# Cross attention: exponentials head by head from the score banks, with the maximum as bias and the sums as a by-product

## The reference

```
def _L1_xattn_ref(query, key, value, Wq, bq, Wk, bk, Wv, bv, Wo, bo, ln_gamma, ln_beta):
    N_HEAD, MODEL_DIM, KEY_DIM, VALUE_DIM = (16, 256, 64, 64)
...
    residual = query
    q = (query @ Wq + bq).reshape(b, sq, N_HEAD, KEY_DIM)
    k = (key @ Wk + bk).reshape(b, key.shape[1], N_HEAD, KEY_DIM)
    v = (value @ Wv + bv).reshape(b, value.shape[1], N_HEAD, VALUE_DIM)
    scores = jnp.einsum('bqhd,bkhd->bhqk', q, k) / TEMP
    attn = jax.nn.softmax(scores, axis=-1)
    out = jnp.einsum('bhqk,bkhd->bqhd', attn, v).reshape(b, sq, N_HEAD * VALUE_DIM)
    out = out @ Wo + bo + residual
    mu = jnp.mean(out, axis=-1, keepdims=True)
    var = jnp.var(out, axis=-1, keepdims=True)
    return (out - mu) * jax.lax.rsqrt(var + EPS) * ln_gamma + ln_beta
```

## Time and profile before

| | |
|---|---|
| median of three runs | 976.95 us (976.56 to 977.26) |
| profiled execution, its time | 975.6 us |
| its span | 973.8 us |
| TensorE busy in the span | 839.3 us, 86% |
| weight loads | 698.3 us, 72% |
| VectorE | 603.9 us, 62% |
| ScalarE | 398.8 us, 41% |
| GpSimd | 223.8 us, 23% |
| mean granted TensorE clock | 0.944 of 2.4 GHz |

### The profile page before, as it was taken

How to read it: one execution, slowest core, us unless ns; L and a number is a source line. 1 busy time by engine, 2 the same in 40 slices (tenths; PEclk the granted TensorE clock), 3 DMA queues, 4 the chain that set the end, 5 groups by cost and what they waited for, 6 DMA issues and landing times.

```text
span 973.8 us, 14784 instructions
## 1 busy us (share of the span) xinstructions
PE 839.3 (86%) x4805; PEld 698.3 (72%) x4806; DVE 603.9 (62%) x1275; ACT 398.8 (41%) x815; POOL 223.8 (23%) x324
## 2 busy tenths in 40 slices
PE   4777999988689999967899979999997059999996
PEld 3456888755578886644788858888886059999996
DVE  4565888747468887573677668899984403333332
ACT  1555667636456765234455523333331002222321
POOL 3771000035300000200001113555453521111111
PEclk9997999999779999989899989999999579999999
DMA  9100000000000000611000073000000264554540
GB/s 290 38 1 0 1 2 1 1 1 1 1 1 1 1 1 1 224 42 52 18 0 0 1 243 103 1 0 1 1 1 1 93 234 144 174 195 166 181 141 8
DMA packets 31624, 57.54 MB, mean 59 GB/s; under 512 B 3285, under 2 KB 22517, under 8 KB 31445
## 3 DMA queue, kind: packets, MB, share of 16 engines
q1 hardware_dynamic: 28339, 49.41, 15.6%
q0 software_dynamic: 2640, 7.30, 2.1%
q10 hardware_dynamic: 594, 0.19, 0.1%
HBM read 47.06 MB, written 8.21 MB: 57 GB/s over the span
## 4 chain that ended last, share of the span: by engine, by line
PE 63%; DVE 17%; issue 6%; ACT 5%; POOL 5%; DMA 2%; SPq 1%; DVEq 0%; ACTq 0%; POOLq 0%
PE PS L1867 9%; PE PS L700 8%; PE PS L1878 8%; PE PS L744 6%; PE PS L1152 4%; PE PS L1286 4%; PE PS L757 3%; PE PS L758 3%; PE PS L1306 2%; PE PS L732 2%; PE PS L575 2%; DVE sum L1394 2%; DVE mx L1386 2%; POOL sorted L1735 2%; PE PS L1297 1%
## 5 line engine op out<-in xcount | busy, mean ns | idle before, releaser
L831 DVE TENSOR_TENSOR PL<-PS,PH 128x512 fp32r<-128x512 f32 x144 | 97.9, 687 | 39.7 <-ACT PH L900 39.2
L900 ACT ACTIVATE PH<-PS 128x512 fp32r<-128x512 f32 x144 | 84.4, 595 | 58.8 <-PE PS L744 57.7
L744 PE MATMUL PS<-ident,prob 128*128 128x128 f32 (+1 forms) x576 | 92.9, 286 | 4.2 <-DVE PL L831 4.0
L891 ACT ACTIVATE prob<-PS,nmax 128x1101 f32<-128x1101 f32 x64 | 75.5, 1180 | 44.8 <-DVE nmax L816 29.4
L1867 PEld LDWEIGHTS PS<-xeT,w 128*128 128x128 f32 x736 | 87.2, 195 | 3.5 <-issue 1.3
L1867 PE MATMUL PS<-xeT,w 128*128 128x128 f32 x736 | 87.6, 278 | 1.9 <-ACT xeT L1827 1.9
L744 PEld LDWEIGHTS PS<-ident,prob 128*128 128x128 f32 (+1 forms) x576 | 66.9, 145 | 28.8 <-DVE PL L831 21.5
L700 PE MATMUL PS<-KH,QS 128*128 128x78 f32 (+1 forms) x182 | 75.1, 413 | 13.8 <-ACT prob L891 12.9
L1878 PE MATMUL PS<-w,hT 128*128 x368 | 83.1, 379 | 0.0
L1878 PEld LDWEIGHTS PS<-w,hT 128*128 128x128 f32 x368 | 68.2, 190 | 8.4
L1306 PE MATMUL PS<-vw,pcT 128*128 128x256 f32 (+1 forms) x320 | 72.9, 383 | 1.2 <-ACT pcT L1496 1.2
(11 more groups left out here) (265 smaller groups left out, 1865.2 us busy)
## 6 DMA issues: line engine op xcount, KB each, us to landing
w<-in_L_ffn_W SPq DMA_DIRECT2D x31, 1024.0 KB, 5.4
xe<-sorted SPq DMA_DIRECT2D x23, 130.0 KB, 2.1
XR<-in_x SPq DMA_DIRECT2D x4, 512.0 KB, 9.1
sorted<-fill POOLq DMA_DIRECT2D x1, 1560.0 KB, 12.4
sorted<-fill POOLq DMA_DIRECT2D x1, 1430.0 KB, 9.3
vw<-vwn SPq DMA_DIRECT2D x14, 77.0 KB
wk<-in_L_xattn_Wk SPq DMA_DIRECT2D x1, 1024.0 KB, 8.7
wv<-in_L_xattn_Wv SPq DMA_DIRECT2D x1, 1024.0 KB, 10.9
```

The source lines that it names most:

```text
L744: last = pe.transpose(PS[0:key_rows(j), bank_of(m, j), s * P:s * P + P], prob[:, m % 2, s, j * P:j * P + key_rows(j)], ident[:])
L831: dve.tensor_tensor(PL[0:r, at, :], PS[0:r, bank_of(m, j), :], PH[0:r, at, :].bitcast(F32), ALU.subtract) \
L891: act.activation(prob[:, m % 2, s, :], PSf[:, at:at + KEYS], ACT.Exp, bias=nmax[:, m % 2, s:s + 1], accum_out=lsum[:, m % 3, s:s + 1]).the ...
L900: act.activation(PH[0:r, at, :], PS[0:r, bank_of(m, j), :], ACT.Copy).then_inc(tile_high, 1)
```

## The change

Nothing of what is computed changes, only where. The names `sc_read` and one of the two counts on `c_sum` go.

- The scores are split at whole heads once: banks of 462, 512 and 258 columns (`SPLIT`, `score_at`). Heads 0 to 5 fill bank 1. Heads 6 to 15 start at bank 2 and run on into bank 3 without a gap, so that head 12 lies across both banks.
- VectorE computes only the negated maxima (`negative_max`); both subtractions are gone.
- ScalarE computes the exponential of each head by an instruction of its own, from PSUM, 77 columns, with `mx1` as bias and `sum1` as accumulated output: 16 a tile instead of 2. The last of a part signals `pexp_ready`.
- VectorE's two sums are gone; it starts with the reciprocals once `pexp_ready` is there.
- The scores of the next tile wait for `pexp_ready` of the tile before, since ScalarE is now the last to read the banks.

The diff, without the lines that only rename:

```
-    SCORES = [(c0, min(c0 + 512, HK)) for c0 in range(0, HK, 512)]
+    HEADS_A = 512 // C
+    SPLIT = HEADS_A * C
+    SCORES = [(0, SPLIT), (SPLIT, SPLIT + 512), (SPLIT + 512, HK)]
+    score_at = lambda h: 512 + h * C if h < HEADS_A else 1024 + (h - HEADS_A) * C
...
         def scores(n, b, p):
             pe.wait_ge(c_zT_low, n + 1)
             if exists(n - 1):
-                pe.wait_ge(sc_read, 2 * n)
+                pe.wait_ge(pexp_ready, 2 * n)
...
-        def subtract_max(n, p, part):
+        def negative_max(n, p, part):
             h0, h1 = PARTS[part]
-            sc = PSf[:, 512 + h0 * C:512 + h1 * C].rearrange("p (h c) -> p h c", c=C)
-            pr = pc[:, p, h0 * C:h1 * C].rearrange("p (h c) -> p h c", c=C)
+            sc = PSf[:, score_at(h0):score_at(h0) + (h1 - h0) * C].rearrange("p (h c) -> p h c", c=C)
             dve.wait_ge(sc_done, 2 * n + part + 1)
-            dve.tensor_reduce(mx1[:, p, h0:h1], sc, AX.X, ALU.max).then_inc(c_max, 1)
-            dve.wait_ge(c_max, 2 * n + part + 1)
-            dve.tensor_tensor(pr, sc, by_head(mx1, p, h0, h1), ALU.subtract).then_inc(sc_read, 1)
+            dve.tensor_reduce(mx1[:, p, h0:h1], sc, AX.X, ALU.max, negate=True).then_inc(c_max, 1)
 
         def divide_by_sum(n, p, part):
             h0, h1 = PARTS[part]
             pr = pc[:, p, h0 * C:h1 * C].rearrange("p (h c) -> p h c", c=C)
             dve.wait_ge(pexp_ready, 2 * n + part + 1)
-            dve.tensor_reduce(sum1[:, p, h0:h1], pr, AX.X, ALU.add).then_inc(c_sum, 1)
-            dve.wait_ge(c_sum, 4 * n + 2 * part + 1)
             dve.reciprocal(sum1[:, p, h0:h1], sum1[:, p, h0:h1]).then_inc(c_sum, 1)
             if part == 1:
-                dve.wait_ge(c_sum, 4 * n + 2 * part + 2)
+                dve.wait_ge(c_sum, 2 * n + 2)
                 dve.tensor_tensor(pr, pr, by_head(sum1, p, h0, h1), ALU.mult).then_inc(pnorm_ready, 1)
...
         def numerators(n, p, part):
             h0, h1 = PARTS[part]
-            act.wait_ge(sc_read, 2 * n + part + 1)
-            pr = pc[:, p, h0 * C:h1 * C]
-            act.activation(pr, pr, ACT.Exp).then_inc(pexp_ready, 1)
+            act.wait_ge(c_max, 2 * n + part + 1)
+            for h in range(h0, h1):
+                last = act.activation(pc[:, p, h * C:h * C + C], PSf[:, score_at(h):score_at(h) + C], ACT.Exp,
+                                      bias=mx1[:, p, h:h + 1], accum_out=sum1[:, p, h:h + 1])
+            last.then_inc(pexp_ready, 1)
```

More of the change, by code:

```diff
@@ L343, in layers_kernel @@
          "y_done lif_step lif_done")
-    (c_bn, c_stats, c_var, c_rstd, c_z, c_zT, c_zT_ready, c_zT_low, c_zb, x_beta, sc_done, c_max, sc_read,
+    (c_bn, c_stats, c_var, c_rstd, c_z, c_zT, c_zT_ready, c_zT_low, c_zb, x_beta, sc_done, c_max,
      pexp_ready, c_sum, pnorm_ready, tp_done, tp_act, pvc_done, res_ready, r_bn, r_stats, r_var, r_rstd,
@@ L348, in layers_kernel @@
      x3_once, x3_kept) = sems(
-         "c_bn c_stats c_var c_rstd c_z c_zT c_zT_ready c_zT_low c_zb x_beta sc_done c_max sc_read pexp_ready "
+         "c_bn c_stats c_var c_rstd c_z c_zT c_zT_ready c_zT_low c_zb x_beta sc_done c_max pexp_ready "
          "c_sum pnorm_ready tp_done tp_act pvc_done res_ready r_bn r_stats r_var r_rstd r_own "
@@ L1245, in dve_ffn @@
         spike(NG - 1, [1])
-    SCORES = [(c0, min(c0 + 512, HK)) for c0 in range(0, HK, 512)]
+    HEADS_A = 512 // C
+    SPLIT = HEADS_A * C
+    SCORES = [(0, SPLIT), (SPLIT, SPLIT + 512), (SPLIT + 512, HK)]
+    score_at = lambda h: 512 + h * C if h < HEADS_A else 1024 + (h - HEADS_A) * C
     TB = S // P
     PAIRS = TB // 2
-    HEADS_A = 512 // C
     PARTS = [(0, HEADS_A), (HEADS_A, H1)]
@@ L1446, in body @@
             if exists(n + 1):
-                subtract_max(n + 1, 1 - p, 0)
-                subtract_max(n + 1, 1 - p, 1)
+                negative_max(n + 1, 1 - p, 0)
+                negative_max(n + 1, 1 - p, 1)
                 divide_by_sum(n + 1, 1 - p, 0)
@@ L1463, in dve_cross @@
         for part in range(2):
-            subtract_max(0, 0, part)
+            negative_max(0, 0, part)
         cross_z_low(dve, 1, 1)
@@ L1542, in divide_first @@
             pr = pc[:, p, h0 * C:h1 * C].rearrange("p (h c) -> p h c", c=C)
-            pool.wait_ge(c_sum, 4 * n + 2)
+            pool.wait_ge(c_sum, 2 * n + 1)
             pool.tensor_tensor(pr, pr, by_head(sum1, p, h0, h1), ALU.mult).then_inc(pnorm_ready, 1)
@@ L1615, in pe_route @@
         pe.wait_ge(x3T_ready, NT)
-        pe.wait_ge(sc_read, 2 * NT)
+        pe.wait_ge(pexp_ready, 2 * NT)
         pe.wait_ge(const_set, 7)
```

## The result

The changed kernel takes 980.25 us (median of 20 runs), the kernel before 976.74 (20 runs). The medians are 3.5 us apart. The ratio is taken of the means of the fast runs, nineteen of each kernel; one execution of each was far slower. It is 1.0031, with an interval of 1.0017 to 1.0046: 3.0 us slower. Forecast were 18 us.

A forecast was written before the change was run, and what follows sets the result against it. VectorE's in-order chain plus rest (6.37 + 4.58 = 10.95 us) was taken to bound, TensorE's 10.77 close below. 15.0 + 1.5 + 0.8 + 0.8 = 18.1 us gave 993.7 profiled, 995.0 beside the median; range 982 to 1010.

The forecast's parts named there:

- the last tile: Tile 15 of cross attention: thirty filler transposes hold TensorE until 739.84, 9.54 us after 730.30, so the 7.83 us chain adds nothing.
- I take 0.364: ScalarE's heads: 0.364 us from one exponential's start to the next, 0.224 to the read-out and 0.14 from there.
- lower bound: ScalarE's heads: 0.224 us to the read-out plus 0.09 until the next instruction, 0.314 from head to head.
- the forecast 7.83: Chain from maximum A to the end of VectorE's multiplication, sixteen exponentials in a row: 7.83 us, against 6.37 before.
- the rest of VectorE's tile: VectorE's work from the multiplication's end to the next maximum A: between 4.08 and 4.58 us, middle 4.33.
- a cheaper rest: VectorE, no longer sharing time with GpSimd, always does its rest in 4.08 us; 3 us fall away; no chance given.
- The start: First tiles of cross attention, counted apart: tile 0 +1.5 us, tiles 1 and 2 +0.8 us each.
- The milder one: Rival on ScalarE's heads: read-outs followed after 0.09 us, +0.45 us a tile, 984 us; chance 14%.
- The page's rule: ScalarE's exponential with pointer bias: 344 ns, 251 from start to start, read-out unpriced; chain 6.07 us, TensorE sets the period.
- not slower: Rival: read-outs hide, heads start 0.25 us apart, TensorE's 10.77 ends the period; 972.6, or 974 beside the median; chance 6%.
- The harsher rival: The read-out drains ScalarE: at 0.44 us a head 1012 us, at 0.51 about 1027; chance 12%.
- the clock inside the warm tiles: Rival: TensorE idles 1.4 us in each 12, its granted clock falls, +13 us on top, 1008 us; chance 5%.

The follow-up runs named there:

- the run with two wide exponentials: Changed kernel with two exponentials a tile from PSUM (462 and 770 columns), without bias, maximum subtraction or sums: 969.71 us, ratio 0.9923 to the kernel before.

## Why the prediction was right and wrong

**Right.** The exponentials became a link of VectorE's chain, because its next instruction waits for them; the chain grew, TensorE waits for the multiplication, the period is chain plus rest; the banks cost nothing; the last tile is hidden behind the fillers. The sign and its reason hold: slower by 3.0 us, with 1 outside the interval. The margin of the sign was small, 0.21 a tile, and not the 1.25 of the sum.

**The step that failed** is one term of the sum: "I take 0.364, because it is a distance between two of the very same instructions." It was, but of two instructions that each waited for VectorE. The right row was the one that the prediction used as its lower bound (160.69 to 160.78, 0.09 behind the read-out), which gave 0.314. Fifteen distances of 0.30 instead of 0.364 are 0.96 us less; the last head with its read-out took 0.50 instead of 0.41, the hand-overs 0.04 and 0.03 instead of 0.06 each. Together the chain of 6.92 is 0.91 shorter than the forecast 7.83.

**The smaller step**: the rest of VectorE's tile, put at 4.33 as the middle of two rows, was 4.12 in the mean of the twelve tiles, seven of them at 3.9 to 4.0 and four at 4.6. That is near the 4.08 that the prediction named as "a cheaper rest"; whether its reason, GpSimd, is the right one was not tested. Over the same tiles the chain is 6.95 in the mean, since tile 3 still has 7.35. The chain is thus 0.88 short of the forecast and the rest 0.21, together the missing 1.09 of the period (12.16 against 11.07). Over the twelve tiles 15.0 us were forecast and 2.5 came; this accounts for 12.5 of the 15 us by which the whole sum was too high.

**The start**: tile 0 was forecast at +1.5. Its chain is 6.92 instead of 6.33, +0.6, and the first period was shorter than before, 12.90 against 13.30, as TensorE left the low clock sooner after its restart: about 4.7 us behind the start of the first turn (granted 0.77 from 576 to 577 us), against 5.9 in the kernel before (0.53 from 577 to 578). In the run with a wait before each head, otherwise the same, that period was 13.14, so a part of this may be chance. Tile 1 was forecast at +0.8: its chain is 7.87 against 7.85. Tile 2's is 7.44 against 7.06. Of the 3.1 us forecast for the start, hardly any came.

**The rivals.** The milder one named the right mechanism at 0.314 a head and gave 984; with 14% it had too little of the chance, and the range ended 2 us above the result. The page's rule (the Trainium skill, "ScalarE: Activation LUTs", section "What ACT_TABLE_LOAD costs") gave 344 ns an exponential and 251 from start to start; the traces show 0.32 to 0.33 for the first heads and 0.21, so here it is above the measurement on both. The read-out that it does not price adds 0.09. The rival that stands on this rule, not slower, named as its threshold a distance of about 0.28, and 0.30 is on the slower side of it by little. The harsher rival and the clock inside the warm tiles did not come: the granted clock was 1.00 in the stretches above.

**What the prediction did not see** is the third of three loops that lie close together. It had VectorE's at 10.95 and TensorE's own at 10.77, but not the one through scores, maximum B and multiplication. A sign of it stood in the earlier trace rows, where maximum B waits eight times for the scores; in those tiles the chain of the kernel before is 6.66 to 7.07 and not 6.37. It came to bound when the first was shortened.

## What to carry to other kernels

A distance between two instructions is a price only where nothing else released the second: compare its start with the end of the work that it waits for, also where no idle time is listed. To move work to an idle engine gains only if the busy engine has something to do meanwhile; here the move lost 3 us, gained 2.8 where only part A moved, and gained 3 to 4 once VectorE's own norms stood under ScalarE's heads and the maxima came bank by bank. Before hoping for more, measure the floor with a version in which the disputed work costs nearly nothing.

## What the runs showed of the hardware

- A read-out of the accumulator lasts 0.19 to 0.29 us in the trace, but delays the next exponential by only 0.09.
- In a row of sixteen such pairs the durations rise, 0.33 for the first exponential and 0.41 for the last, while the starts stay 0.30 apart; at the next row they begin at 0.33 again. Without read-outs they rise too, to 0.43 for the sixteenth, while the starts stay 0.21 apart. The recorded duration of one is not what one more costs.
- A semaphore wait that is already satisfied before each of the heads changed their distance by nothing that the trace resolves.
- With 6.1 us without matmuls in tile 0 (6.8 in the change) TensorE's granted clock fell to 0.50, 1.2 GHz, before the matmuls resumed, and came back to 1.00, 2.4 GHz, 4.7 to 5.9 us after; with transposes in the gap it stayed at 1.00. In the run with two wide exponentials the gap was 3.65 us, and the clock fell to 0.50 only after they had resumed.
